# Score matmuls of a gated cross-attention block, addressed as 64-row array tiles

## The chip, the cores and the metric

The kernel runs on one core of one Trainium2 chip. The metric is the device time of one execution in microseconds (us), as the median of several runs. All arrays are float32.

## The reference

The reference is one block of a Flamingo-like model: layer norm, cross-attention to a context with a small feed-forward, a gated residual, layer norm, a top-2 mixture of eight experts with a shared one, a gated residual. B=4, N=512 query rows, 1601 context rows, width 256, context width 192, 16 heads of 16.

```python
def xattn(x, y):                      # x (4,512,256) normalised, y (4,1601,192)
    q = (x @ Wq + bq).reshape(B, N, 16, 16)
    k = (y @ Wk + bk).reshape(B, M, 16, 16)
    v = (y @ Wv + bv).reshape(B, M, 16, 16)
    scores = einsum('bnhd,bmhd->bhnm', q, k) / 4
    attn = softmax(scores, axis=-1)
    out = einsum('bhnm,bmhd->bnhd', attn, v).reshape(B, N, 256)
    return relu(out @ W1 + b1) @ W2 + b2
x = x + tanh(g_xattn) * xattn(layernorm(x), ctx)
x = x + tanh(g_ffn) * moe(layernorm(x))   # shared + top 2 of 8 experts, silu-gated, 256 -> 512 -> 256
```

## The kernel before

The kernel has two blocks, `attention` and `experts`; the change lies in the first. Attention works through 16 **units**, each one batch element and four heads, and each unit through 13 **steps**, one key tile of 128 context rows each: 208 steps.

**Stacks.** The scores are computed in fp32r with a high and a low part of q and k. For each pair p of heads, `kst` holds three parts of 16 rows for head 2p from partition 0 on and for head 2p+1 from partition 64 on (`[128, 2, 1604]`, filled with ones outside the parts), and `qst` the query side, one plane per head (`[128, 4, 512]`), with zeros in the rows of the other head, so that a matmul over all 128 rows gives one head's scores. Row 48 of a head's part (`STK`) takes the negated row maximum of q, against the ones of `kst`. Three buffers of each rotate (`NKB`). `load_stacks` on SP's queue writes them by 28 small DMAs a unit: 12 for kst (L310), 12 for qst (L312), and 4 that set row 48 to zero from `zrow` (L317). `load_rows` (L324) writes the maxima later.

**Two passes over the scores.** First, `S` jobs (L488): for each head, query tile t and key quarter q, 128 queries by 402 keys into one bank of the four-bank `ring`, 64 chunks a unit; VectorE takes the maximum of each (L677) and frees the slot. Then a `MX` job transposes the maxima, which go to row 48. Second, `st` (L542): 128 keys by 512 queries of one head into one of the three banks `st_ps`; ScalarE writes the exponential to `probs` (L442). `pv` (L554) multiplies the four heads' `probs` of a step by the values, on four column tiles of 32, into one accumulating bank `pv_ps`, with a column of ones for the denominator.

**Order.** `schedule()` writes the order by hand. The chunks of unit u+1 are spread over the steps of unit u, five in most steps, shifted by LEAD = 3 steps; the chunks of unit 0 and the first 15 of unit 1 stand in the prologue. The other jobs (K, Q, V projections and transposes XT of the next batch element; SUM, DIV, W1, W2 of the last) are put in fixed steps and all use the ring, in one order of slots: job n waits until job n-4 is freed. In a step TensorE's order is: chunk, st h0, chunk, st h1, chunk, st h2, `pv` of the step before, chunk, st h3, then what is left of the chunks, then the others.

```python
def st(u, mt, h):                                    # L536
    if idx >= NST:
        pe.wait_ge(exp_done, idx - NST + 1)          # three banks
def pv(m):                                           # L545
    pe.wait_ge(exp_done, 4 * (m + 1))                # all four heads of its step
```

In the K and V jobs the contraction over the context's width 192 is split in 128 and 64 rows. SP's queue works in its own order (L334 to L346): at the start of unit u the stacks of u+2, then `pack(u-1)` (L295), which W1 waits for, then the maxima of u+1.

Of the kernel before, what the change touches and what calls it, by code (L numbers as in the profile page):

```python
# [22 lines left out]
F32 = mybir.dt.float32  # L23
# [52 lines left out]
def schedule():  # L76

    def proj(b):
        return ([("XT", b, dt) for dt in range(2)] + [("Q", b, dt) for dt in range(2)],
                [("K", b, dt, q) for dt in range(2) for q in range(4)],  # L80
                [("V", b, g) for g in range(VJOBS)])

    def scores(u):
        return [("S", u, h, t, q) for h in range(4) for t in range(NT) for q in range(4)]


    qj, k, v = proj(0)

    prologue = k + qj + v + scores(0) + [("MX", 0)]
    jobs = [[] for _ in range(UNITS * MT)]  # L90
    for u in range(1, UNITS):
        chunks, start = scores(u), MT * (u - 1) - LEAD
        for n, chunk in enumerate(chunks):
            at = start + n * MT // len(chunks)
            if at < 0:
                prologue.append(chunk)
            else:
                jobs[at].append(chunk)
        jobs[start + MT].append(("MX", u))
    for u in range(UNITS):  # L100
        b, hg = divmod(u, 4)
        extra = {}
        if u > 0:
            extra[1], extra[2] = [("SUM", u - 1)], [("DIV", u - 1)]
        if u == UNITS - 1:
            for n in range(B - 1):
                extra[7 + 2 * n] = [("XT2", n, 0), ("XT2", n, 1)]
                extra[8 + 2 * n] = [("LG", n)]
        if hg == 0 and b > 0:
            for f in range(F1 // P):  # L110
                extra[5 + f] = [("W1", b - 1, f)]
            extra[10], extra[11] = [("W2", b - 1, 0)], [("W2", b - 1, 1)]
        if b + 1 < B:
            qj, k, v = proj(b + 1)
            if hg == 1:
                extra[3], extra[5], extra[6] = qj[0:2], qj[2:3], qj[3:4]
                for n in range(5):
                    extra[8 + n] = k[n:n + 1]
            if hg == 2:
                extra[0] = k[5:6]  # L120
                extra[1], extra[3] = extra[1] + k[6:7], k[7:8]
                for n in range(VJOBS):
                    extra[4 + n] = v[n:n + 1]
        for mt, more in extra.items():
            jobs[MT * u + mt] += more

    steps = [(m // MT, m % MT, sorted(jobs[m], key=lambda job: job[0] != "S")) for m in range(UNITS * MT)]
    b = B - 1
    epilogue = ([("SUM", UNITS - 1), ("DIV", UNITS - 1)] + [("W1", b, f) for f in range(F1 // P)] +
                [("W2", b, 0), ("W2", b, 1)])  # L130
    return prologue, steps, epilogue
# [47 lines left out]
def attention(nc, I, x1, stats, mv, veps, power, rstd, tg, ident, xg_dram,  # L179
# [19 lines left out]
    with ExitStack() as ctx:  # L199
# [26 lines left out]
        kc = parts[:, 4 * N:4 * (N + MP)].rearrange("p (t c n) -> p t c n", t=2, c=2).bitcast(F32R)  # L226
        vp = sb("vp", [P, 2, MT, H, VW])
        kst = [sb(f"kst{i}", [P, 2, MP], F32R) for i in range(NKB)]
        qst = [sb(f"qst{i}", [P, 4, N], F32R) for i in range(NKB)]
        zrow = sb("zrow", [4, P])  # L230
        zeros = sb("zeros", [P, D])
        mpart = sb("mpart", [P, 4, NT, 4])
        mx = sb("mx", [P, 4, NT])
# [29 lines left out]
        zeroed = sem("zeroed")  # L263

        QK_LOADS, W_LOADS = 5, 11
        STACK_LOADS = 16 * 2 * 7
        block = ctx.enter_context(nc.Block())

        @block.sync
        def _(sp):  # L270
# [26 lines left out]
            def load_stacks(u):  # L297
                b, hg = divmod(u, 4)

                sp.wait_ge(ring_free, max(count(("K", b, 1, 3)), count(("Q", b, 1))))  # L300
                if u >= NKB:
                    sp.wait_ge(st_full, 4 * MT * (u - NKB + 1))
                for p in range(2):
                    loaded = stack_loaded[u % NKB][p]
                    for j in range(2):
                        head = 4 * hg + 2 * p + j
                        dt, r = head // 8, HD * (head % 8)
                        for g, (qpart, kpart) in enumerate(((0, 0), (0, 1), (1, 0))):
                            at = 64 * j + HD * g
                            sp.dma_start(kst[u % NKB][at:at + HD, p, :].bitcast(F32),  # L310
                                         kc[r:r + HD, dt, kpart, :].bitcast(F32)).then_inc(loaded, 16)
                            sp.dma_start(qst[u % NKB][at:at + HD, 2 * p + j, :].bitcast(F32),  # L312
                                         qc[r:r + HD, dt, qpart, :].bitcast(F32)).then_inc(loaded, 16)


                        at = 64 * j + STK
                        sp.dma_start(qst[u % NKB][at:at + 1, 2 * p + j, :].rearrange("o (t n) -> o t n", n=P).bitcast(F32),  # L317
                                     zrow[:]).then_inc(loaded, 16)

            def load_rows(u):  # L320
                sp.wait_ge(ring_free, count(("MX", u)))
                for h in range(4):
                    at = 64 * (h % 2) + STK
                    sp.dma_start(qst[u % NKB][at:at + 1, h, :].rearrange("o (t n) -> o t n", n=P).bitcast(F32),  # L324
                                 mneg[NT * h:NT * (h + 1), :].bitcast(F32)).then_inc(row_loaded[u % NKB], 16)

            sp.wait_ge(pool_ready, 5)
# [24 lines left out]
        def _(pool):  # L352
# [6 lines left out]

            nc.gpsimd.affine_select(out=sel[:], in_=sel[:], compare_op=ALU.not_equal, fill=1.0, base=-HD,  # L360
                                    pattern=[[-32, 4]], channel_multiplier=1).then_inc(pool_ready, 1)
            nc.gpsimd.memset(zrow[:], 0.0)
            nc.gpsimd.memset(zeros[:], 0.0)
            nc.gpsimd.memset(vp[:, :, :, :, HD:VW].rearrange("p c m h o -> p (c m h) o"), 1.0)
            for i in range(NKB):
                nc.gpsimd.memset(qst[i][:].bitcast(F32), 0.0)
                last = nc.gpsimd.memset(kst[i][:].bitcast(F32), 1.0)
            last.then_inc(pool_ready, 1)
            def make_rstd(b):
# [81 lines left out]
        def _(pe):  # L451
            def do(job):
# [31 lines left out]
                elif kind == "S":  # L484
                    _, u, h, t, q = job
                    if h % 2 == 0 and (t, q) == (0, 0):
                        pe.wait_ge(stack_loaded[u % NKB][h // 2], STACK_LOADS * (u // NKB + 1))
                    last = nc.tensor.matmul(slot[:, 0:SCH], qst[u % NKB][:, h, t * P:(t + 1) * P],  # L488
                                            kst[u % NKB][:, h // 2, score_at(q):score_at(q) + SCH],
                                            start=True, stop=True)  # L490
                elif kind == "MX":
                    pe.wait_ge(mx_ready, job[1] + 1)
# [43 lines left out]
            def st(u, mt, h):  # L536
# [2 lines left out]
                    pe.wait_ge(row_loaded[u % NKB], 64 * (u // NKB + 1))  # L539
                if idx >= NST:  # L540
                    pe.wait_ge(exp_done, idx - NST + 1)
                nc.tensor.matmul(st_ps[0:w, idx % NST, :], kst[u % NKB][:, h // 2, mt * P:mt * P + w],  # L542
                                 qst[u % NKB][:, h, :], start=True, stop=True).then_inc(st_full, 1)

            def pv(m):  # L545
                u, mt = divmod(m, MT)
# [15 lines left out]
            for u, mt, jobs in steps:  # L562

                chunks = [job for job in jobs if job[0] == "S"]
                others = [job for job in jobs if job[0] != "S"]
                for h in range(4):
                    if h == 3 and MT * u + mt > 0:
                        pv(MT * u + mt - 1)
                    for job in chunks[h:h + 1]:
                        do(job)  # L570
                    st(u, mt, h)
                for job in chunks[4:] + others:
                    do(job)
            pv(MT * UNITS - 1)
            for job in epilogue:
# [577 lines left out]
```

## Time and profile before

| | us |
|---|---|
| median of 3 runs | 1333.47 |
| lowest, highest | 1330.21, 1335.7 |
| span of the profiled execution | 1354.8 |
| TensorE busy in it (5662 matmuls) | 1254.9 |
| VectorE busy | 749.8 |
| ScalarE busy | 546.8 |

The profile is of one execution, which with a span of 1354.8 us is longer than the median of the runs by 21 us; of its own time outside the span nothing is recorded. PE is TensorE's matmuls, PEld its weight loads, DVE VectorE, ACT ScalarE, POOL GpSimd, SPq the DMA issues of the sync engine. A matmul's recorded duration contains its way through the array, so that matmuls which follow one on another overlap in the record; the distance between their starts is what each holds the engine. "Idle before" is the engine's idle time ahead of an instruction, with what ended it. The lines of the view by rows join instructions of one group that stand close to each other.

### The profile page before, as it was taken

How to read it: one execution, taken by the hardware profiler on the slowest of the kernel's cores; microseconds unless marked ns; L12 is line 12 of the kernel's file. 1: busy time of each engine (PE TensorE's matmuls, PEld its weight loads, DVE VectorE, ACT ScalarE, POOL GpSimd, SP SyncE). 2: the span in 40 equal slices, each digit the busy share in tenths (PEclk: the TensorE clock that was granted, in tenths of full speed). 3: DMA queues.
4: the chain of work that ended last, by engine and by line, in shares of the span. 5: the costliest groups of instructions: out<-in, count | busy, mean ns of one | idle time of the engine just before them, and what ended most of it. 6: DMA issues, size and time to landing. Idle time of an engine off the chain costs nothing. (4 is left out here: it accounts for less than half of the span.)

```text
span 1354.8 us, 16247 instructions
## 1 busy us (share of the span) xinstructions
PE 1254.9 (93%) x5662; PEld 704.1 (52%) x5662; DVE 749.8 (55%) x1624; ACT 546.8 (40%) x1004; POOL 97.3 (7%) x114
## 2 busy tenths in 40 slices
PE   6899999999999999999999999997858999999982
PEld 2455545555645555554555565544434555555551
DVE  1498776686776588576668778632601222222244
ACT  1006564564555366346456547771201111111110
POOL 4000000000000000000000000000170000000044
PEclk9959999999999999899999999997988999999996
DMA  9344403323210453040322421010850111111124
GB/s 308 45 68 71 53 1 47 63 37 51 28 26 1 53 90 49 5 53 1 41 32 34 53 30 24 5 51 4 297 184 31 32 46 40 39 48 39 39 71 124
DMA packets 53840, 78.43 MB, mean 58 GB/s; under 512 B 13312, under 2 KB 38912, under 8 KB 53760
## 3 DMA queue, kind: packets, MB, share of 16 engines
q1 hardware_dynamic: 47744, 67.01, 24.9%
q0 software_dynamic: 3072, 8.39, 1.9%
q10 hardware_dynamic: 2944, 1.98, 0.5%
q8 instruction: 47, 0.77, 0.2%
q14 instruction: 33, 0.27, 0.1%
HBM read 32.47 MB, written 16.52 MB: 36 GB/s over the span
## 5 line engine op out<-in xcount | busy, mean ns | idle before, releaser
L442 ACT ACTIVATE probs<-st_ps 128x512 f32<-128x512 f32 (+1 forms) x832 | 450.5, 598 | 361.8 <-PE st_ps L542 360.6
L677 DVE TENSOR_REDUCE mpart<-ring 128x1 f32<-128x402 f32 x1024 | 521.3, 568 | 85.0 <-PE ring L488 83.0
L488 PE MATMUL ring<-kst,qst 128*128 128x402 f32 x1024 | 389.1, 406 | 0.8 <-DVE xnT L637 0.3
L542 PE MATMUL st_ps<-qst,kst 128*128 128x512 f32 (+1 forms) x832 | 327.7, 400 | 1.9 <-ACT probs L442 1.8
L488 PEld LDWEIGHTS ring<-kst,qst 128*128 128x128 f32 x1024 | 200.1, 196 | 215.1 <-DVE mpart L677 175.9
L554 PE MATMUL pv_ps<-probs,vp 128*17 128x512 f32 (+1 forms) x1664 | 219.6, 600 | 0.1
L542 PEld LDWEIGHTS st_ps<-qst,kst 128*128 128x128 f32 (+1 forms) x832 | 154.0, 187 | 41.8 <-ACT probs L442 19.5
L845 ACT ACTIVATE s_sb<-gu_ps 128x512 f32<-128x512 f32 x55 | 32.9, 598 | 304.8 <-PE gu_ps L920 252.5
L920 PE MATMUL gu_ps<-wgu,xbT 128*128 x312 | 144.1, 604 | 7.4 <-issue 7.3
L1049 DVE TENSOR_TENSOR h_sb<-s_sb,gu_ps 128x512 f32<-128x512 f32 x55 | 37.8, 687 | 204.0 <-ACT s_sb L845 184.0
L920 PEld LDWEIGHTS gu_ps<-wgu,xbT 128*128 128x128 f32 x312 | 56.1, 189 | 78.5 <-issue 78.5
L473 PE MATMUL ring<-cold,wk 64*128 64x401 f32 (+1 forms) x128 | 67.3, 633 | 10.2 <-DMA bq<-in_bq 10.2
L939 PE MATMUL y_ps<-wd,hT 128*128 x312 | 73.9, 380 | 0.0
L382 POOL COPY rspread<-rden 128x512 f32<-128x512 f32 x16 | 9.8, 616 | 841.6 <-DVE rden L688 841.6
L939 PE MATMUL y_ps<-cold,hT 128*128 128x256 f32 x128 | 37.3, 443 | 31.6 <-DVE x L1063 17.9
L482 PE MATMUL ring<-wv,cold 128*128 128x256 f32 (+1 forms) x208 | 64.2, 417 | 0.0
L920 PE MATMUL gu_ps<-cold,parts 128*128 128x512 f32 x128 | 60.7, 620 | 2.0 <-PEq L199 2.0
L554 PEld LDWEIGHTS pv_ps<-probs,vp 128*17 128x17 f32 (+1 forms) x1664 | 27.6, 95 | 66.2 <-ACT probs L442 57.0
L939 PEld LDWEIGHTS y_ps<-wd,hT 128*128 128x128 f32 x312 | 56.2, 190 | 6.0
L656 DVE SCALAR_TENSOR_TENSOR parts<-ring,bk,parts 128x401 fp32r<-128x401 f32 x32 | 20.3, 635 | 59.3 <-ACT parts L427 59.3
L835 POOL DMA_INDIRECT y_back<-sorted_y,slot_i x32 | 31.2, 975 | 295.4 <-DMA sorted_y<-ysb 279.1
L928 PEld LDWEIGHTS ht_ps<-ident,h_sb 128*128 128x128 f32 x220 | 27.7, 142 | 38.0 <-issue 27.4
(125 smaller groups left out, 716.2 us busy)
## 6 DMA issues: line engine op xcount, KB each, us to landing
kst<-parts SPq DMA_DIRECT2D x192, 100.2 KB
qst<-parts SPq DMA_DIRECT2D x192, 32.0 KB
sorted_x<-zeros SPq DMA_DIRECT2D x1, 4992.0 KB, 16.4
xb<-sorted_x SPq DMA_DIRECT2D x39, 128.0 KB, 2.1
sorted_y<-ysb SPq DMA_DIRECT2D x39, 128.0 KB, 1.7
wgu<-in_WgT SPq DMA_DIRECT2D x16, 256.0 KB, 6.7
wgu<-in_WuT SPq DMA_DIRECT2D x16, 256.0 KB, 7.1
wd<-in_WdT SPq DMA_DIRECT2D x8, 512.0 KB, 8.4
```

Of the source, the lines that this page charges most:

```text
L442: nc.scalar.activation(probs[0:w, m % NPB, h, :], st_ps[0:w, (4 * m + h) % NST, :], ACT.Exp, scale=SCALE).then_inc(exp_done, 1)
L473: last = nc.tensor.matmul(slot[:, 0:KCH], w[:, dt * P:(dt + 1) * P], c[:, q * KCH:(q + 1) * KCH], start=(k == 0), stop=(k == 1))
L482: last = nc.tensor.matmul(slot[0:w, i * D:(i + 1) * D], c[:, mt * P:mt * P + w], wv[:, :], start=(k == 0), stop=(k == 1))
L488: last = nc.tensor.matmul(slot[:, 0:SCH], qst[u % NKB][:, h, t * P:(t + 1) * P], kst[u % NKB][:, h // 2, score_at(q):score_at(q) + SCH], s ...
L542: nc.tensor.matmul(st_ps[0:w, idx % NST, :], kst[u % NKB][:, h // 2, mt * P:mt * P + w], qst[u % NKB][:, h, :], start=True, stop=True).the ...
L554: last = nc.tensor.matmul(pv_ps[32 * h:32 * h + VW, :], vp[0:w, b % 2, mt, 4 * hg + h, :], probs[0:w, m % NPB, h, :], start=(mt == 0), sto ...
L677: last = nc.vector.tensor_reduce(mpart[:, h, t, q:q + 1], slot[:, 0:SCH], AX.X, ALU.max)
L835: pool.indirect_dma_start(yg[:, n % NYG, c, :], None, yg_dram[:], bass.IndirectOffsetOnAxis(ap=slot_i[:, c, t:t + 1], axis=0)).then_inc(ga ...
L845: nc.scalar.activation(s_sb[:, i % 2, :], gu_ps[:, i % 2, 0, :], ACT.Silu).then_inc(silu_done, 1)
L920: last = nc.tensor.matmul(gu_ps[:, i % 2, f, :], x, w, start=(k == 0), stop=(k == 1))
L939: last = nc.tensor.matmul(y_ps[:, 0:D], hT[:, i % 2, k, :], w, start=(k == 0), stop=(k == FK - 1))
L1049: nc.vector.tensor_tensor(h_sb[:, i % 2, :], s_sb[:, i % 2, :], gu_ps[:, i % 2, 1, :], ALU.mult).then_inc(h_ready, 1)
```

## The change

Query stacks of a pair of heads now share one plane, `qst` is `[128, 2, 512]`, with head 2p in rows 0 to 47 (48 with the maximum) and head 2p+1 in rows 64 to 111 (112). Every score matmul names only its head's rows: 48 in `S`, which leaves row 48 out, and 49 in `st`. So they are addressed to the array's 64-row tiles at row 0 and row 64. The zero rows, the zeroing DMAs and the memset of `qst` are gone. The chunks of a pair of heads alternate between the two, and in a step the order is: two chunks, st h0 and h1, two chunks, st h2 and h3, the chunks left, `pv` of the step before, the others. The chunks' size, their banks and VectorE's maxima are as before.

```diff
     def scores(u):
-        return [("S", u, h, t, q) for h in range(4) for t in range(NT) for q in range(4)]
+        return [("S", u, 2 * p + j, t, q) for p in range(2) for t in range(NT) for q in range(4) for j in range(2)]
...
-        qst = [sb(f"qst{i}", [P, 4, N], F32R) for i in range(NKB)]
-        zrow = sb("zrow", [4, P])
+        qst = [sb(f"qst{i}", [P, 2, N], F32R) for i in range(NKB)]
...
-        STACK_LOADS = 16 * 2 * 7
+        STACK_LOADS = 16 * 2 * 6
...
-                        at = 64 * j + STK
-                        sp.dma_start(qst[u % NKB][at:at + 1, 2 * p + j, :].rearrange("o (t n) -> o t n", n=P).bitcast(F32),
-                                     zrow[:]).then_inc(loaded, 16)
...
             for i in range(NKB):
-                nc.gpsimd.memset(qst[i][:].bitcast(F32), 0.0)
...
-                    last = nc.tensor.matmul(slot[:, 0:SCH], qst[u % NKB][:, h, t * P:(t + 1) * P],
-                                            kst[u % NKB][:, h // 2, score_at(q):score_at(q) + SCH],
+                    at = 64 * (h % 2)
+                    last = nc.tensor.matmul(slot[:, 0:SCH], qst[u % NKB][at:at + STK, h // 2, t * P:(t + 1) * P],
+                                            kst[u % NKB][at:at + STK, h // 2, score_at(q):score_at(q) + SCH],
                                             start=True, stop=True)
...
-                nc.tensor.matmul(st_ps[0:w, idx % NST, :], kst[u % NKB][:, h // 2, mt * P:mt * P + w],
-                                 qst[u % NKB][:, h, :], start=True, stop=True).then_inc(st_full, 1)
+                at = 64 * (h % 2)
+                rows = slice(at, at + STK + 1)
+                nc.tensor.matmul(st_ps[0:w, idx % NST, :], kst[u % NKB][rows, h // 2, mt * P:mt * P + w],
+                                 qst[u % NKB][rows, h // 2, :], start=True, stop=True).then_inc(st_full, 1)
...
-                for h in range(4):
-                    if h == 3 and MT * u + mt > 0:
-                        pv(MT * u + mt - 1)
-                    for job in chunks[h:h + 1]:
+                for p in range(2):
+                    for job in chunks[2 * p:2 * p + 2]:
                         do(job)
-                    st(u, mt, h)
-                for job in chunks[4:] + others:
+                    for j in range(2):
+                        st(u, mt, 2 * p + j)
+                for job in chunks[4:]:
+                    do(job)
+                if MT * u + mt > 0:
+                    pv(MT * u + mt - 1)
+                for job in others:
                     do(job)
```

TensorE's order in plain steps of unit 0, before (chunks are `ring<-kst,qst`, key-major scores `st_ps<-qst,kst`, weighted values `pv_ps<-probs,vp`):

```order
49 L554 MATMUL pv_ps<-probs,vp 17x512 x4
50 L488 MATMUL ring<-kst,qst 128x402
51 L542 MATMUL st_ps<-qst,kst 128x512
52 L488 MATMUL ring<-kst,qst 128x402 x2
53 L542 MATMUL st_ps<-qst,kst 128x512
54 L488 MATMUL ring<-kst,qst 128x402
55 L542 MATMUL st_ps<-qst,kst 128x512
56 L488 MATMUL ring<-kst,qst 128x402
57 L542 MATMUL st_ps<-qst,kst 128x512
58 L554 MATMUL pv_ps<-probs,vp 17x512 x4
```

and after the change:

```order
41 L549 MATMUL pv_ps<-probs,vp 17x512 x4
42 L481 MATMUL ring<-kst,qst 128x402 x2
43 L537 MATMUL st_ps<-qst,kst 128x512 x2
44 L481 MATMUL ring<-kst,qst 128x402 x2
45 L537 MATMUL st_ps<-qst,kst 128x512 x2
46 L481 MATMUL ring<-kst,qst 128x402
47 L549 MATMUL pv_ps<-probs,vp 17x512 x4
```

Between two pv groups stand the same five chunks and four key-major matmuls; before, the first of the latter behind pv was h3 of the step, and now all four of a step stand together.

TensorE's order around a K projection (`ring<-cold,wk`) in unit 1, before:

```order
214 L554 MATMUL pv_ps<-probs,vp 17x512 x4
215 L488 MATMUL ring<-kst,qst 128x402
216 L542 MATMUL st_ps<-qst,kst 128x512
217 L488 MATMUL ring<-kst,qst 128x402
218 L473 MATMUL ring<-cold,wk 128x401 x2
219 L488 MATMUL ring<-kst,qst 128x402
220 L542 MATMUL st_ps<-qst,kst 128x512
```

and after:

```order
141 L481 MATMUL ring<-kst,qst 128x402
142 L549 MATMUL pv_ps<-probs,vp 17x512 x4
143 L465 MATMUL ring<-cold,wk 128x401 x2
144 L481 MATMUL ring<-kst,qst 128x402 x2
145 L537 MATMUL st_ps<-qst,kst 128x512 x2
```

The projection stood behind h3 and the last chunk, with pv before those; now pv stands directly before it.

## Rows read from the trace of the kernel before

**Rows 1.** Windows: us, busy (x) of PE, PEld, DVE, ACT, POOL, PEclk, DMA

```profile
286.00:307.00 21.00, 21.00 (x120) 11.51 (x119) 17.43 (x37) 14.93 (x29) 0.00 (x0) 1.00 0.12 14
888.00:912.00 24.00, 23.13 (x143) 11.14 (x146) 12.30 (x43) 17.36 (x33) 3.17 (x3) 1.00 0.03 6
```

**Rows 2.** The page's costliest groups: xcount | busy us, mean ns | idle before

```profile
L442 ACT ACTIVATE probs<-st_ps 128x512 f32<-128x512 f32 (+1 forms) x832 | 450.5, 598 | 361.8 <-PE st_ps L542 360.6
L677 DVE TENSOR_REDUCE mpart<-ring 128x1 f32<-128x402 f32 x1024 | 521.3, 568 | 85.0 <-PE ring L488 83.0
```

**Rows 3.** Timeline of a plain step, unit 3: start us, us, engine, line

```profile
289.28 0.13 PEld L554 LDWEIGHTS pv_ps<-probs,vp 128*17 128x17 f32 x8 [0.32 <-ACT probs L442]
289.28 1.05 PE L554 MATMUL pv_ps<-probs,vp 128*17 128x512 f32 x8
290.26 0.19 PEld L488 LDWEIGHTS ring<-kst,qst 128*128 128x128 f32 x1 [0.85 <-DVE mpart L677]
290.37 0.19 PEld L542 LDWEIGHTS st_ps<-qst,kst 128*128 128x128 f32 x1
290.55 0.39 PE L542 MATMUL st_ps<-qst,kst 128*128 128x512 f32 x1
...
290.98 1.68 ACT L442 ACTIVATE probs<-st_ps 128x512 f32<-128x512 f32 x3 [0.84 <-PE st_ps L542]
...
291.38 0.34 PE L488 MATMUL ring<-kst,qst 128*128 128x402 f32 x1
...
291.56 0.39 PE L542 MATMUL st_ps<-qst,kst 128*128 128x512 f32 x1
...
291.79 0.35 PE L488 MATMUL ring<-kst,qst 128*128 128x402 f32 x1
...
291.98 0.39 PE L542 MATMUL st_ps<-qst,kst 128*128 128x512 f32 x1
292.29 0.13 PEld L554 LDWEIGHTS pv_ps<-probs,vp 128*17 128x17 f32 x8 [0.31 <-ACT probs L442]
```

**Rows 4.** Timeline of a step with a K projection, unit 2

```profile
217.61 0.29 PEld L473 LDWEIGHTS ring<-cold,wk 64*128 64x128 f32 x2 [0.57 <-issue]
218.48 0.19 PEld L488 LDWEIGHTS ring<-kst,qst 128*128 128x128 f32 x1 [0.57 <-issue]
...
219.28 0.63 DVE L656 SCALAR_TENSOR_TENSOR parts<-ring,bk,parts 128x401 fp32r<-128x401 f32 x1 [1.59 <-ACT parts L427]
```

**Rows 5.** Timeline of the prologue, VectorE's chunks of unit 0

```profile
64.25 31.03 DVE L677 TENSOR_REDUCE mpart<-ring 128x1 f32<-128x402 f32 x64
```

**Rows 6.** Timeline of a step without chunks, unit 15

```profile
898.39 2.07 ACT L442 ACTIVATE probs<-st_ps 128x512 f32<-128x512 f32 x4 [0.52 <-PE st_ps L542]
899.04 0.19 PEld L542 LDWEIGHTS st_ps<-qst,kst 128*128 128x128 f32 x1 [0.66 <-ACT probs L442]
...
899.47 0.13 PEld L554 LDWEIGHTS pv_ps<-probs,vp 128*17 128x17 f32 x8 [0.24 <-ACT probs L442]
```

**Rows 7.** Groups by line: VectorE's work on W2

```profile
L701 DVE TENSOR_TENSOR ytmp<-ring,b 128x256 f32<-128x256 f32 x16 | 6.0, 419 | 21.0 <-PE ring L532 21.0
```

**Rows 8.** Timeline of SP's queue, unit 4

```profile
303.10 0.56 SPq L310 DMA_DIRECT2D kst<-parts  x1
...
320.84 0.63 SPq L317 DMA_DIRECT2D qst<-zrow  x1
321.51 2.41 SPq L295 DMA_DIRECT2D onc<-on  x4
```

**Rows 9.** Who waited for whom: us in total, times, longest us

```profile
PE ring L524 <- DMA onc<-on: 11.0, 4, 4.6
...
PE ring L462 <- DVE xn L606: 9.2, 4, 2.8
```

**Rows 10.** Windows, columns as in rows 1: behind W1's wait, unit 8

```profile
544.60:551.40 6.80, 6.15 (x14) 3.32 (x18) 2.22 (x4) 1.27 (x3) 0.00 (x0) 0.50 0.00 1
```

**Rows 11.** Timeline of TensorE in unit 1, at the lower clock

```profile
160.89 1.71 PE L554 MATMUL pv_ps<-probs,vp 128*17 128x512 f32 x8
```

More of the change, by code:

```diff
@@ L311, in load_stacks @@
                                          kc[r:r + HD, dt, kpart, :].bitcast(F32)).then_inc(loaded, 16)
-                            sp.dma_start(qst[u % NKB][at:at + HD, 2 * p + j, :].bitcast(F32),
+                            sp.dma_start(qst[u % NKB][at:at + HD, p, :].bitcast(F32),
                                          qc[r:r + HD, dt, qpart, :].bitcast(F32)).then_inc(loaded, 16)
-                        at = 64 * j + STK
-                        sp.dma_start(qst[u % NKB][at:at + 1, 2 * p + j, :].rearrange("o (t n) -> o t n", n=P).bitcast(F32),
-                                     zrow[:]).then_inc(loaded, 16)
             def load_rows(u):
@@ L323, in load_rows @@
                     at = 64 * (h % 2) + STK
-                    sp.dma_start(qst[u % NKB][at:at + 1, h, :].rearrange("o (t n) -> o t n", n=P).bitcast(F32),
+                    sp.dma_start(qst[u % NKB][at:at + 1, h // 2, :].rearrange("o (t n) -> o t n", n=P).bitcast(F32),
                                  mneg[NT * h:NT * (h + 1), :].bitcast(F32)).then_inc(row_loaded[u % NKB], 16)
@@ L361, in _ @@
                                     pattern=[[-32, 4]], channel_multiplier=1).then_inc(pool_ready, 1)
-            nc.gpsimd.memset(zrow[:], 0.0)
             nc.gpsimd.memset(zeros[:], 0.0)
```

## The prediction

> **What bounds the kernel now.** I first read windows [rows 1]. In a stretch of plain steps of the attention loop (208 steps: 16 units of 13 key tiles) TensorE is busy all of 21 us, VectorE 17.4, ScalarE 14.9. The prologue is touched in little and the experts not at all, so the loop decides. The costliest groups [rows 2] are the two that read the scores: VectorE reduces the chunks (L677), ScalarE exponentiates the key-major tiles (L442, 598 ns); TensorE makes them in L488 and L542 and multiplies with the values in L554 (pv).
>
> The timeline of one plain step [rows 3] has no hole on TensorE. From one pv group (289.28) to the next (292.29) it is 3.01 us: pv holds the engine for 0.98 (289.28 to 290.26), and nine matmuls follow one on another. A score chunk takes 0.18 (291.38 to 291.56), a key-major one 0.23 (291.56 to 291.79), each load (PEld) under the matmul before it. At pv's two edges something is lost: pv starts 0.32 after the last key-major matmul, not 0.23, and the first chunk behind it needs 0.29 instead of 0.18, as its load (290.26) could not run early: the next load starts 0.11 after it (290.37). I read this as the price of a change of tile shape: about 0.10 at the end of the old shape and 0.11 for an uncovered load, 0.2 together. The K projection confirms it inside a job: its 64-row half changes shape, its load starts only at 217.61, and the first chunk's load behind it again only at 218.48 [rows 4].
>
> VectorE takes a chunk every 0.48 (31.03 us for 64 in the prologue [rows 5]), 2.4 a step. ScalarE takes a tile about every 0.5. So TensorE is the bound by about 0.6 us a step, and the question is what its program order makes wait once it is faster.
>
> **The change part by part. 1: the plain step.** Two matmuls on rows 0 and 64 use different halves of the array and write different banks, so I expect them to run together. TensorE's own work would fall from 3.01 to about 2.1. But the new order has a chain in it. The key-major matmul h3 must wait for the exponential of h0 (three banks), and pv, which used to fill that wait, now stands behind h3. This chain is priced from the steps without chunks [rows 6], where it shows today. Start at the first chunk's load behind pv: loads one behind another each 0.11 put h0 at 0.33; from a key-major start to its exponential 0.43 (290.55 to 290.98 [rows 3]); exponential 0.60; its end (898.39 + 0.60) to the next load 0.05 (899.04); that load to pv 0.43 (899.04 to 899.47); pv 0.98. Sum 2.82. In about every second step the five chunks begin on row 64, since five is odd. Then the second chunk shares h0's rows (h0 at 0.40) and the fifth shares h3's and runs behind it (0.17): 3.06. Mean 2.94 against 3.01, that is -0.07 in the 192 steps that have chunks: **-13 us**.
>
> The unknown is whether the two halves' loads run together. The nearest rows both ways: 0.11 apart (full array), or hardly apart, as pv's eight loads on four column tiles, which take 0.13 in all. With the second, h0 is at 0.29 and pv earlier: 2.78 and 2.95, -0.14 a step. If nothing overlaps at all, h0 starts at 0.29 + 0.18 = 0.47, the step is 2.96, and the fifth chunk's 0.18 on top makes 3.14: +0.13. I take the first, since here too both loads bring 128 columns each, and keep the others for the range.
>
> The Trainium skill (page "TensorE: Matmul & The Clock Gate", section "The mechanism") says that loads and matmuls on different row groups start about 4 ns apart. By it the step would be the second value, 2.87. No row of this trace has two row tiles in flight, so the rule is a rival below.
>
> **2: changes of shape.** K and V end in their 64-row half. Today they cost: into 64 rows, and out of it to the full array. After the change the chunk that follows is in 64-row shape already; but pv now stands before them, another edge only if they need the full array first. Counted over a step, K had four edges (chunk to pv, pv to chunk, into, out of) and will have three (to pv, pv to K, K's inner one): -0.2 in the 45 steps with K or V in the written order, **-9 us**. Jobs in the full array alone (SUM, DIV, MX, Q, W1, W2, XT) stand in 57 other steps with chunks; they had two edges and get three: **+11 us**. V alternates twice and still saves one.
>
> **3: the ring.** All five chunks of a step now stand before its pv, and there are four ring slots. The fifth chunk waits until VectorE has reduced the first one of the same step. In a plain step it has (0.29 + 0.2 + 0.48, under 1.5). Behind K it hasn't: K's low part ends on VectorE 1.43 after K's end (219.28 + 0.63 against 218.48 [rows 4]), the first chunk's reduction 0.48 later, so the fifth chunk starts at about 1.95 and pv at about 2.35, where the chain alone has pv at 1.84 to 2.08. I take 0.45 for 24 K steps (+11). Q's two passes are 0.1 longer each: 0.6 for 6 (+3.5). Behind W2 VectorE has two adds of 0.42 [rows 7] and two operations of the same shape: fifth chunk at 2.4, 0.65 for 6 (+4). **+18 us**. Ends: 0 if ScalarE and VectorE come sooner, +30. Today the fourth and fifth chunk come behind pv and wait for none of this.
>
> **4: the last unit.** Its steps have no chunks; today SUM, DIV, the second transposes and LG fill the wait for the exponential (0.66 of idle before the load at 899.04 [rows 6]). Now they stand outside it. Eight or nine such jobs at 0.4 to 0.7: **+5 us**.
>
> **5: waits that shrink.** SP issues 28 stack transfers at the start of a unit, 18.4 us (303.10 to 321.51), and only then the pack that W1 waits for [rows 8]. Four of them, the zero rows (0.63 each), go: 2.6 earlier. And pv, 0.98, now runs before W1 instead of behind it. Together 3.6. The list of waits has W1 four times behind the pack, 11.0 in all [rows 9]; the longest, 4.6, is the epilogue's, so units 4, 8 and 12 share 6.4, none of them over 3.6: -6.5. Behind the wait in unit 8 the granted clock is 0.50 for 6.8 us [rows 10]; without two such dips I take -4. XT's wait for the normalised rows (up to 2.8 [rows 9], three times in the loop) has pv before it and saves about 1 each: -3.5. **-14 us**. The memsets of qst and zrow on POOL gate only the first stack transfers, which wait for the K and Q projections anyway: nothing. The other 16 x 4 zero-row transfers lie under other work; in the prologue VectorE's 0.48 per chunk is the bound [rows 5]: nothing. Were that cover gone, each transfer would cost its 0.63.
>
> Sum: -13 - 9 + 11 + 18 + 5 - 14 = **-2 us**. The profiled execution spans 1354.8, 21 above the median 1333.47; the terms are differences of durations at full clock, so I take them off the median: **1331 us**. Here 0.5% (6.7 us) is about what a measurement can tell from no change.
>
> **The rivals.** *Loads together.* The halves' loads overlap as pv's do: another -0.07 in the 159 steps without the ring's wait, -11: **1320 us**. For it: pv's loads, and the skill's sentence. Against: pv's have 17 columns each.
>
> *No overlap, the slower side.* Row tiles run one behind another (a shared read path or load buffer). Then only the order has changed: the chain plus the serial chunks, 0.20 more than the forecast in those 159 steps: +32, **1363 us**. It decides as soon as a pair of key-major matmuls starts over 0.15 apart. For it: full-array matmuls never overlap here. Against: pv's four column tiles do (eight matmuls of 512 columns in 1.05, where eight at 0.23 would take 1.84). This is also the case in which the change doesn't do what it says.
>
> *The clock.* TensorE will idle about 0.45 a step. If the grant fell to 1.2 GHz in a third of the loop, a step would cost about 1.1 more (pv alone 1.71 instead of 1.05 at 160.89 [rows 11]): +70, **1400 us**. Against: in the last unit it waits 0.66 in each step of 2.6 and has 1.00 granted [rows 1].
>
> **How the numbers follow.** Forecast 0.60 (own range 1314 to 1345: the ring term from 0 to 30 and term 5), loads together 0.20, no overlap 0.12, clock 0.05, else 0.03. Range 1306 to 1364: loads together with a small ring term at the low end, no overlap at the high. Faster by over 0.5%: a third of the forecast and most of the second case, 0.35. Within: half the forecast and some of the second, 0.35. Slower: the rest of the forecast, no overlap, clock: 0.30.
>
> **What would show it.** In the plain steps of the new trace: pairs of L481 and of L537 with starts 0.11 apart or less; a hole before each h3, ended by ScalarE; steps of 2.8 and 3.05 in turn. In K steps the fifth chunk released by VectorE. W1 without a wait for the pack. VectorE and ScalarE groups unchanged in mean. Plain steps under 2.7 would mean that the chain is not what I think; over 3.1, that nothing overlaps.

## The result and the profile after

| | before | changed |
|---|---|---|
| median, us | 1332.74 (4 runs) | 1439.94 (4 runs) |
| lowest, highest | 1330.21, 1335.7 | 1423.31, 1446.3 |
| ratio | | 1.075, 95% interval 1.069 to 1.082 |
| span of the profiled execution | 1354.8 | 1444.6 |
| mean granted clock in it | 0.958 | 0.866 |

The change is slower by 7.5%, 107 us by the medians, and outside the range that was given. The profiled execution of the changed kernel is the slowest of its four; the others have a mean granted clock of 0.871 to 0.884. The spans of the two profiles differ by less than the medians, since the experts behind the loop took 18 us more in that of before, from the same instructions. In the traces of all runs below they take either 412 to 416 or 431 to 434 us, whatever the kernel, so this is no effect of the change. The attention loop alone, by windows of the two traces (columns: us, then busy and count of PE, PEld, DVE, ACT and POOL, granted clock, DMA share, GB/s), before:

```profile
107.00:922.00 815.00, 799.98 (x4193) 443.95 (x4189) 570.25 (x1183) 471.04 (x871) 14.33 (x21) 0.99 0.25 36
```

and changed, with two stretches out of it, one of unit 7 and one that begins two steps before unit 13 and ends in it:

```profile
109.00:1030.00 921.00, 852.10 (x4190) 378.43 (x4186) 563.20 (x1182) 454.40 (x871) 14.27 (x21) 0.84 0.22 32
549.90:583.40 33.50, 30.64 (x198) 12.49 (x196) 29.48 (x60) 24.29 (x48) 0.00 (x0) 1.00 0.17 24
874.20:935.60 61.40, 61.40 (x235) 25.12 (x227) 33.71 (x69) 26.08 (x51) 0.61 (x1) 0.50 0.22 29
```

The loop is 106 us longer, the whole loss. Its granted clock is 0.84 instead of 0.99. As the grant has two levels, 1.2 and 2.4 GHz, a mean c says that the share 2(1-c) was spent at the lower: 0.32 of 921, about 295 us, against 16 before (with two digits of c, such figures are good to about 9 us either way). The two stretches hold plain steps in the main (the second also those with SUM and DIV): at 2.4 GHz 60 VectorE operations pass in 33.5 us (0.56 each), at 1.2 GHz 69 in 61.4 (0.89). Plain steps alone say the same. In the second stretch, from one pv group to the next:

```profile
895.39 1.91 PE L549 MATMUL pv_ps<-probs,vp 128*17 128x512 f32 x8
900.10 1.91 PE L549 MATMUL pv_ps<-probs,vp 128*17 128x512 f32 x8
904.47 1.91 PE L549 MATMUL pv_ps<-probs,vp 128*17 128x512 f32 x8
```

They take 4.71 and 4.37 in turn, 4.54 on average, against 2.87 at the full clock (below). So a us at the lower level loses 0.37 us, 295 lose 109, and that is the loss. At the full clock the changed loop would take about 812, and that of before 809, by the same sum.

A plain step of it in unit 7, timeline at the full clock (start us, us, engine, line):

```profile
564.28 0.19 PEld L481 LDWEIGHTS ring<-kst,qst 48*128 48x128 f32 x2 [0.85 <-DVE mpart L675]
564.28 0.46 PE L481 MATMUL ring<-kst,qst 48*128 48x402 f32 x2
564.39 0.19 PEld L537 LDWEIGHTS st_ps<-qst,kst 49*128 49x128 f32 x2
564.57 0.40 PE L537 MATMUL st_ps<-qst,kst 49*128 49x512 f32 x2
...
565.00 2.06 ACT L434 ACTIVATE probs<-st_ps 128x512 f32<-128x512 f32 x4 [0.72 <-PE st_ps L537]
565.65 0.18 PEld L537 LDWEIGHTS st_ps<-qst,kst 49*128 49x128 f32 x1 [0.65 <-ACT probs L434]
565.65 0.49 PE L537 MATMUL st_ps<-qst,kst 49*128 49x512 f32 x1 [0.27 <-ACT probs L434]
565.76 0.19 PEld L481 LDWEIGHTS ring<-kst,qst 48*128 48x128 f32 x1
565.99 0.34 PE L481 MATMUL ring<-kst,qst 48*128 48x402 f32 x1
566.26 0.13 PEld L549 LDWEIGHTS pv_ps<-probs,vp 128*17 128x17 f32 x8 [0.31 <-ACT probs L434]
566.26 1.05 PE L549 MATMUL pv_ps<-probs,vp 128*17 128x512 f32 x8
567.24 0.19 PEld L481 LDWEIGHTS ring<-kst,qst 48*128 48x128 f32 x2 [0.85 <-DVE mpart L675]
```

Two key-major matmuls take 0.40 in one record, where a single one has 0.39 [rows 3] and two on the full array have 0.62 (run 1 below); the two chunks behind pv take 0.46 with their uncovered load, where run 1 has 0.64; two loads take 0.19, as one does. So the pair runs together, loads too. From first load to first load it is 2.96 us; the next step of the same trace takes 2.78 (567.24 to 570.02). The chain is there link by link: h0 at 0.29, its exponential 0.43 later (565.00), the load of h3 at 565.65 with 0.65 of idle before it that ScalarE ended, pv 0.61 later, 0.98 for pv.

The groups that answer to [rows 2], and TensorE's three, on the changed kernel's page:

```profile
L434 ACT ACTIVATE probs<-st_ps 128x512 f32<-128x512 f32 (+1 forms) x832 | 433.5, 600 | 426.6 <-PE st_ps L537 426.3
L675 DVE TENSOR_REDUCE mpart<-ring 128x1 f32<-128x402 f32 x1024 | 513.4, 568 | 61.1 <-PE ring L481 59.9
L481 PE MATMUL ring<-kst,qst 48*128 48x402 f32 x1024 | 348.2, 479 | 36.3 <-DVE parts L654 20.3
L549 PE MATMUL pv_ps<-probs,vp 128*17 128x512 f32 (+1 forms) x1664 | 265.3, 715 | 0.0
```

ScalarE's and VectorE's means are as before (600 and 568 ns). Those of TensorE grew with the clock: pv was not touched, and its mean is 715 ns. Where the grant falls shows in a step that has SUM, unit 8, timeline:

```profile
584.44 1.05 PE L490 MATMUL ring<-sel,osb 128*128 128x4 f32 x8
...
587.42 1.90 PE L549 MATMUL pv_ps<-probs,vp 128*17 128x512 f32 x8
```

SUM moves 4 columns eight times in 1.05 us; the pv at the end of this step already takes 1.90 instead of 1.05. This is one place of many: other stretches at the lower level begin where no SUM stands near (the longest, from 874.20 on, 10 us before the SUM of unit 13 at 884.34).

### The profile page after: what moved, and what is told of

It reads as the page before. It is cut to its first block and busy times, and to the rows that moved or that the text cites. A ratio compares the mean times of both kernels' runs of the same rounds, so it can differ in the third digit from the quotient of the medians.

```text
span 1444.6 us, 16179 instructions
## 1 busy us (share of the span) xinstructions
PE 1305.0 (90%) x5662; PEld 637.3 (44%) x5662; DVE 743.5 (51%) x1624; ACT 530.2 (37%) x1004; POOL 91.6 (6%) x110
## 5 line engine op out<-in xcount | busy, mean ns | idle before, releaser
L434 ACT ACTIVATE probs<-st_ps 128x512 f32<-128x512 f32 (+1 forms) x832 | 433.5, 600 | 426.6 <-PE st_ps L537 426.3
L481 PE MATMUL ring<-kst,qst 48*128 48x402 f32 x1024 | 348.2, 479 | 36.3 <-DVE parts L654 20.3
L537 PE MATMUL st_ps<-qst,kst 49*128 49x512 f32 (+1 forms) x832 | 301.2, 474 | 27.8 <-ACT probs L434 27.1
L549 PE MATMUL pv_ps<-probs,vp 128*17 128x512 f32 (+1 forms) x1664 | 265.3, 715 | 0.0
L481 PEld LDWEIGHTS ring<-kst,qst 48*128 48x128 f32 x1024 | 168.8, 215 | 206.4 <-DVE mpart L675 93.1
L537 PEld LDWEIGHTS st_ps<-qst,kst 49*128 49x128 f32 (+1 forms) x832 | 135.5, 209 | 109.4 <-ACT probs L434 96.4
L465 PE MATMUL ring<-cold,wk 64*128 64x401 f32 (+1 forms) x128 | 82.8, 760 | 10.3 <-DMA bq<-in_bq 10.3
L654 DVE SCALAR_TENSOR_TENSOR parts<-ring,bk,parts 128x401 fp32r<-128x401 f32 x32 | 20.3, 635 | 86.3 <-ACT parts L419 86.3
L465 PEld LDWEIGHTS ring<-cold,wk 64*128 64x128 f32 (+1 forms) x128 | 26.8, 261 | 65.0 <-issue 47.2
L474 PEld LDWEIGHTS ring<-wv,cold 128*128 128x128 f32 (+1 forms) x208 | 32.3, 194 | 47.8 <-issue 32.0
L419 ACT ACTIVATE parts<-ring,bk 128x401 fp32r<-128x401 f32 x32 | 19.0, 595 | 85.4 <-PE ring L465 85.3
```

What stands on the lines that cost most here:

```text
L434: nc.scalar.activation(probs[0:w, m % NPB, h, :], st_ps[0:w, (4 * m + h) % NST, :], ACT.Exp, scale=SCALE).then_inc(exp_done, 1)
L465: last = nc.tensor.matmul(slot[:, 0:KCH], w[:, dt * P:(dt + 1) * P], c[:, q * KCH:(q + 1) * KCH], start=(k == 0), stop=(k == 1))
L474: last = nc.tensor.matmul(slot[0:w, i * D:(i + 1) * D], c[:, mt * P:mt * P + w], wv[:, :], start=(k == 0), stop=(k == 1))
L481: last = nc.tensor.matmul(slot[:, 0:SCH], qst[u % NKB][at:at + STK, h // 2, t * P:(t + 1) * P], kst[u % NKB][at:at + STK, h // 2, score_at ...
L537: nc.tensor.matmul(st_ps[0:w, idx % NST, :], kst[u % NKB][rows, h // 2, mt * P:mt * P + w], qst[u % NKB][rows, h // 2, :], start=True, sto ...
L549: last = nc.tensor.matmul(pv_ps[32 * h:32 * h + VW, :], vp[0:w, b % 2, mt, 4 * hg + h, :], probs[0:w, m % NPB, h, :], start=(mt == 0), sto ...
```

## Experiments

Theory A: the loss is TensorE's clock, and it falls because the 64-row tiles leave the array with less work per us. Theory B: the new order brings it, by pv's place and the hole in front of h3.

**1. The order alone.** The kernel before, with only the changed step loop; chunks stay in their order by heads.

```diff
-                for h in range(4):
-                    if h == 3 and MT * u + mt > 0:
-                        pv(MT * u + mt - 1)
-                    for job in chunks[h:h + 1]:
+                for p in range(2):
+                    for job in chunks[2 * p:2 * p + 2]:
                         do(job)
-                    st(u, mt, h)
-                for job in chunks[4:] + others:
+                    for j in range(2):
+                        st(u, mt, 2 * p + j)
+                for job in chunks[4:]:
+                    do(job)
+                if MT * u + mt > 0:
+                    pv(MT * u + mt - 1)
+                for job in others:
                     do(job)
```

> The kernel before (full-array matmuls, its chunk order by heads) with only the new order of a step: two chunks, h0 and h1, two chunks, h2 and h3, the chunks left, pv, the others. Theory A (the time was lost to TensorE's clock, which falls because 64-row tiles leave the array with less work per us): full-array matmuls keep it busy, the loop has under 40 us at 1.2 GHz as before (17), and the time rises only by the order's own chain, a plain step 3.1 instead of 3.01: about 1365 us. Theory B (the new place of pv brings the clock down by its holes): some 200 to 300 us of the loop at 1.2 GHz here too, time over 1420 us.

Measured: ratio 1.024 (1.021 to 1.027), 1387.2 us beside 1355.3 for before on the same chip. Window of its loop:

```profile
108.00:952.00 844.00, 821.85 (x4188) 427.00 (x4186) 561.08 (x1181) 456.29 (x872) 14.28 (x21) 1.00 0.24 35
```

and out of the timeline of a plain step:

```profile
290.82 0.64 PE L488 MATMUL ring<-kst,qst 128*128 128x402 f32 x2
291.29 0.62 PE L542 MATMUL st_ps<-qst,kst 128*128 128x512 f32 x2
...
292.37 0.19 PEld L542 LDWEIGHTS st_ps<-qst,kst 128*128 128x128 f32 x1 [0.25 <-ACT probs L442]
...
293.96 0.64 PE L488 MATMUL ring<-kst,qst 128*128 128x402 f32 x2
```

The clock is full, better than before: the order alone does not bring it down, so Theory B falls. The order has its own price, 29 us of the loop (844 against 815): its plain steps take 3.14 (290.82 to 293.96), which is the value that the prediction gave for the case without overlap, and the load of h3 has the hole before it that ScalarE ends.

**2. The tiles alone.** The changed kernel's tiles, stacks and transfers in the order of before.

```diff
+        return [("S", u, h, t, q) for h in range(4) for t in range(NT) for q in range(4)]
...
+                for h in range(4):
+                    if h == 3 and MT * u + mt > 0:
+                        pv(MT * u + mt - 1)
...
```

> The changed kernel's 64-row tiles and small stacks, with the order of before in both respects (chunks by heads, a chunk and a key-major matmul in turn, pv before h3). Theory A: less array work per us than before, so the clock falls as in the changed kernel, 200 us or more of the loop at 1.2 GHz, over 1400 us. Theory B: the clock stays as before (under 40 us low) and neighbouring tiles overlap where they can: at full clock a plain step of about 2.6, 1280 to 1300 us.

Measured: ratio 0.990 (0.987 to 0.993), 1340.7 beside 1355.3. Window:

```profile
108.00:906.00 798.00, 779.70 (x4189) 378.47 (x4188) 567.51 (x1183) 466.27 (x872) 14.29 (x21) 0.93 0.25 37
```

Neither theory's number came. The clock falls with the tiles alone (about 110 us low), as A says, but by a third of the changed kernel's, and the steps gain more than that costs: the loop is 17 us shorter than before. So it is the tiles that bring the clock down, and tiles and new order together that bring it down so far. By the sum above (0.37 us for each at the lower level) this loop would take about 757 at the full clock, 52 less than that of before; the changed order, at about 812, gives all of it back.

**3. pv back before h3, chunks still in pairs.**

```diff
+                    for j in range(2):
+                        if (p, j) == (1, 1) and MT * u + mt > 0:
+                            pv(MT * u + mt - 1)
+                        st(u, mt, 2 * p + j)
```

> The changed kernel with pv put back before h3, chunks still in pairs. Theory A: TensorE does the same work in shorter steps (2.7 at full clock), so its share of busy time rises somewhat; the clock still falls in part, 1300 to 1400 us. Theory B: no hole before h3, clock as before, about 1290 us.

Measured: 1496.7 and 1533.1 us beside 1355.3, slower by over 10%; both executions are far above the changed kernel's. The profile is that of the longer one, with a mean clock of 0.801; the other had 0.827. Window of its loop, and of plain steps in it at the full clock:

```profile
109.00:1098.00 989.00, 942.17 (x4194) 413.46 (x4196) 569.45 (x1182) 468.24 (x872) 14.31 (x21) 0.74 0.20 30
622.00:649.00 27.00, 25.61 (x170) 10.39 (x169) 24.49 (x51) 20.54 (x40) 0.00 (x0) 1.00 0.16 21
```

A miss for both theories by about 100 us and more. Over half of this loop is at 1.2 GHz. Is idle time what brings the clock down? The lower level itself makes TensorE's busy share larger (61.40 of 61.40 us in the stretch above), so the share has to be compared at the full clock: in plain steps TensorE is busy 25.61 of 27.00 us here (95%) and 30.64 of 33.50 in the changed kernel (91%). Less idle time went with the lower clock, so idle time is not what decides. Why this order is so much worse is open.

**4. Work added.** The changed kernel, each matmul of h2 issued twice into the same bank.

```diff
+                if h == 2:
+                    nc.tensor.matmul(st_ps[0:w, idx % NST, :], kst[u % NKB][rows, h // 2, mt * P:mt * P + w],
+                                     qst[u % NKB][rows, h // 2, :], start=True, stop=True)
```

> The changed kernel with each key-major matmul of h2 issued twice into the same bank (same result), which lies in the hole before h3: 208 matmuls more. Theory A: more array work per us, the clock recovers at least in part: under 200 us of the loop at 1.2 GHz (changed kernel 300), time 1330 to 1400 us although work is added. If instead the loss has another cause than the clock, the added 0.2 us a step costs 0 to 40 us: 1440 to 1480 us.

Measured: ratio 1.034 (1.031 to 1.038), 1401.4 beside 1355.3, against the changed kernel's 1.075. With 208 matmuls more the ratio is lower by 4%, as Theory A had it:

```profile
108.00:965.00 857.00, 809.70 (x4396) 377.87 (x4392) 561.27 (x1181) 457.36 (x871) 14.31 (x21) 0.92 0.23 34
```

About 137 us of it are at the lower level. At the full clock it would take some 806, so the added matmuls cost nothing: they fill the hole before h3.

**5. More rows.** What does "work" mean here? The changed kernel again, with 64 rows named by every score matmul instead of 48 or 49; the rows added hold zeros on the query side and ones on the key side. For that the four zero-row transfers of a unit and the memset of `qst` are back too.

```diff
-                    last = nc.tensor.matmul(slot[:, 0:SCH], qst[u % NKB][at:at + STK, h // 2, t * P:(t + 1) * P],
-                                            kst[u % NKB][at:at + STK, h // 2, score_at(q):score_at(q) + SCH],
+                    last = nc.tensor.matmul(slot[:, 0:SCH], qst[u % NKB][at:at + 64, h // 2, t * P:(t + 1) * P],
+                                            kst[u % NKB][at:at + 64, h // 2, score_at(q):score_at(q) + SCH],
...
-                rows = slice(at, at + STK + 1)
+                rows = slice(at, at + 64)
...
+                        sp.dma_start(qst[u % NKB][at:at + 1, p, :].rearrange("o (t n) -> o t n", n=P).bitcast(F32),
+                                     zrow[:]).then_inc(loaded, 16)
...
+                nc.gpsimd.memset(qst[i][:].bitcast(F32), 0.0)
```

> The changed kernel with the same tiles, order and timing, but each score matmul names 64 rows instead of 48 or 49 (the extra rows hold zeros on the query side; the zero-row transfers and the memset are back). If what holds the clock up is how much of the array takes part, a third more rows must recover part of it: under 200 us of the loop at 1.2 GHz (changed kernel 300), under 1400 us. If only the time counts in which matmuls stream, which halves when two run together, the rows change nothing: 300 us low or somewhat less or more, 1420 to 1460 us.

Measured: ratio 1.011 (1.004 to 1.018), 1351.9 beside 1336.0. Windows of its loop and of a stretch of unit 13, where the changed kernel was at the lower clock:

```profile
107.00:934.00 827.00, 744.73 (x4192) 333.20 (x4194) 561.88 (x1183) 454.21 (x871) 14.27 (x21) 0.97 0.25 35
814.00:849.00 35.00, 32.36 (x212) 13.32 (x210) 30.09 (x62) 24.69 (x49) 0.00 (x0) 1.00 0.19 26
```

TensorE has the same instructions in the same order, and at the full clock the loop would take about 809 beside 812; yet 94 us of it come back: 50 us low instead of 295. TensorE's busy share at the full clock is the same (32.36 of 35.00 us, 92%, against 91%). So the clock follows the rows that the matmuls name, or what the added rows hold; the two are not told apart.

**6. The dose.** 64 rows in the key-major matmuls alone; the chunks keep 48, and no zero rows are transferred.

```diff
+                nc.gpsimd.memset(qst[i][:].bitcast(F32), 0.0)
...
-                rows = slice(at, at + STK + 1)
+                rows = slice(at, at + 64)
```

> The changed kernel with 64 rows in the key-major matmuls alone (the chunks keep 48), 4 x 512 of the 4 x 512 + 5 x 402 columns of a step. With rows as the measure a dose between the changed kernel (300 us low) and rows64 (54): 100 to 220 us low, 1370 to 1410 us. If the zero-row transfers or the later pack of rows64 made its difference instead of the rows, nothing is gained here: 1420 us or more.

Measured: ratio 1.016 (1.007 to 1.024), 1375.8 beside 1353.6. Window of its loop:

```profile
109.00:933.00 824.00, 748.43 (x4190) 334.95 (x4186) 561.27 (x1181) 453.81 (x870) 14.31 (x21) 0.96 0.24 35
```

The gain does not come from the zero-row transfers of run 5. Is it a dose in between? The profiled execution, the faster of two, has 66 us low, less than the 100 expected at least; the other has a mean clock of 0.924 against its 0.940, some 45 us more. By the ratios, four of nine matmuls a step bring all that run 5 brought, as far as two executions of each can tell. The same edit on run 3's kernel, the slowest of all:

> Run rows_pv_mid (506 us of its loop at 1.2 GHz, the slowest of all) with 64 rows instead of 49 in the key-major matmuls. If rows are what decides, most of it comes back here too: under 200 us low, under 1400 us. If that kernel's long stretches at the lower clock have another cause (pv between the key-major matmuls): still over 350 us low, over 1450 us.

Measured: 1372.4 beside 1349.6, ratio 1.017 (1.002 to 1.032), where run 3 had 1.10 to 1.13; this is the outcome that was expected if rows decide. Its loop:

```profile
109.00:945.00 836.00, 774.29 (x4192) 344.32 (x4188) 568.28 (x1181) 464.90 (x870) 14.27 (x21) 0.94 0.24 35
```

The runs stand beside before on the chip of each; the changed kernel itself was measured on one chip alone. Run 3 and its counterpart here were on two chips as well. That the chip should make 0.84 or 0.74 out of 0.96 is not tested away, but before has a mean clock of 0.958 to 0.966 on all of them.

**7. SUM.** The changed kernel with SUM's passes moving 128 columns.

```diff
-                        last = nc.tensor.matmul(slot[:, 4 * t:4 * t + 4], osb[:, t * P:(t + 1) * P],
+                        last = nc.tensor.matmul(slot[:, t * P:(t + 1) * P], osb[:, t * P:(t + 1) * P],
```

with `sel` 128 columns wide and the reciprocal reading four of each 128.

> The changed kernel with SUM's eight passes moving 128 columns instead of 4 (124 of them unused), at the same spacing, since each is bound by its weight load. Theory A: the falls of the clock at the starts of the units, where SUM stands and the array streams nearly nothing for 1 us, go or get shorter; 200 to 250 us of the loop at 1.2 GHz, 1390 to 1430 us. If SUM has nothing to do with it: no difference to the changed kernel beyond 10 us.

Measured: ratio 1.037 (1.022 to 1.053). Window of its loop:

```profile
109.00:962.00 853.00, 779.05 (x4192) 345.16 (x4194) 562.22 (x1182) 453.85 (x871) 14.26 (x21) 0.93 0.23 34
```

Some 120 us are low in this, the faster of two executions (1378.2 and 1395.5 us, mean clocks 0.924 and 0.906). That is more than was expected of one job of 1 us in each unit. How much of it is SUM's own doing isn't shown: low stretches are gone that do not begin behind a SUM (that of 874.20 among them), and in the old order the same edit brings nothing (run 8).

**8. The tiles in the order of before, with the remedies.** First SUM widened alone:

> The 64-row tiles in the order of before (run rows_old_order: 104 us of its loop at 1.2 GHz, 1 per cent faster than the kernel before) with SUM's passes widened to 128 columns. Theory A: its falls behind SUM and DIV in units 8, 13 and 14 (6.8 us each) go, 10 to 15 us less than rows_old_order; 2 per cent faster than the kernel before.

Measured: ratio 0.988 (0.977 to 1.000), loop clock 0.93 as in run 2: SUM brought nothing down there that could be seen, where 10 to 15 us were expected. With the second h2 matmul on top:

> As old_sum_wide, and each key-major matmul of h2 is issued twice. Theory A: the prologue's last stretch and the falls in units 1, 4, 5 and 9 get shorter too, under 60 us low in the loop; against it stands up to 0.2 us a step where TensorE is the bound: between 25 us faster and 20 us slower than old_sum_wide.

Measured: ratio 1.011 (1.000 to 1.022), 30 us slower than old_sum_wide and so outside what was expected. Its loop clock is better (0.95 against 0.93), but in this order no hole takes up the added matmuls, and they cost more than the clock gives. Then the rows, in all score matmuls (without the wide SUM) and in the key-major ones alone (with it):

> The order of before in both respects with 64-row tiles whose matmuls name all 64 rows (zero rows loaded as before). Theory A with rows as its measure (run rows64 had 54 us low instead of 300): the loop of rows_old_order (798 us) loses most of its 104 us at 1.2 GHz, about 40 us less, less the pack's wait that the 28 transfers bring back (7): ratio to the kernel before 0.96 to 0.975, 1280 to 1300 us on a chip where before takes 1333. If the rows' effect was chance: 0.985 to 1.0.

> As old_sum_wide, but the key-major matmuls name 64 rows (the chunks keep 48, so no zero-row transfers). Between old_sum_wide (0.988) and old_rows64: ratio 0.965 to 0.985, 50 to 90 us of the loop at 1.2 GHz.

Measured, three rounds: 0.983 (0.980 to 0.987) and **0.975 (0.970 to 0.979)**, 1332.0 and 1321.1 us beside 1353.6. The first is a smaller gain than expected, close to what was to be called chance (0.985 and above): 64 rows in all score matmuls bring 0.7% against run 2's 0.990, with W1's waits for the pack back. The second lies in its range, is better than the first by more than their intervals, and the best of all; it has the wide SUM and no zero-row transfers. Window of its loop:

```profile
108.00:888.00 780.00, 760.81 (x4194) 370.43 (x4197) 566.76 (x1183) 465.15 (x872) 14.33 (x21) 0.96 0.26 37
```

35 us less than before at a clock that is still below its 0.99. What the tiles save in this order (run 2) makes the larger part of it.

## Why the prediction was wrong

**The step that failed** is the rival called the clock: its chance of 0.05 and the reason against it. The prediction argued from the last unit, where TensorE waits in each step and has 1.00 granted [rows 1]. That row shows full-array matmuls with the same idle time; it says nothing of matmuls on 48 rows. Idle time was the wrong quantity, as runs 3 and 5 show; with 64 rows named, at the same idle time, the loop's clock is 0.97 instead of 0.84. Its price, 1.1 us for a plain step at the lower clock, was too low: 4.54 against 2.87 on average, 1.7. The pv of 1.71 that it was taken from [rows 11] was not at the lower level to its end:

```profile
158.90:162.30 3.40, 3.40 (x13) 0.99 (x12) 2.93 (x9) 1.79 (x3) 1.27 (x2) 0.50 0.49 69
162.40:163.00 0.60, 0.60 (x6) 0.47 (x3) 0.00 (x0) 0.00 (x0) 0.00 (x0) 1.00 0.24 55
```

It ends at 162.60; one wholly at the lower level takes 1.91. The rival's third of the loop was right (0.32), and that was a guess. So its 1400 us became 1440.

**The sum at the full clock** held: the terms gave -2 us, and the loops without their lost clock are about 812 and 809. It held in part by luck, since some terms were off and their errors cancel. With the loads as measured, the plain steps would have brought the sum to -13; K steps took back 3 us of that, and the rest isn't attributed.

- *Plain step*, forecast 2.82 and 3.06 in turn: 2.78 and 2.96. The chain is right in each link; the taken value for the loads was not. They start together (two in 0.19). The Trainium skill (page "TensorE: Matmul & The Clock Gate", section "The mechanism") has loads and matmuls on different row groups overlap, and the trace agrees. The 2.78 and 2.95 worked out for that case are what was measured. In the written terms the rival "loads together" was true and the serial one false. Its time of 1320 was not reached, for the clock.
- *Changes of shape*: right for V. A V step shortened from 5.53 (219.92 to 225.45, before) to 5.27 (501.09 to 506.36) between pv groups, where the terms gave -0.27.
- *The ring*: present and too small, and the job that waits is another one. In the list of waits of the changed kernel K's low part on VectorE ends idle time of loads and matmuls of the chunks; before, such rows do not stand in the list:

```profile
PEld ring L481 <- DVE mpart L675: 93.1, 179, 1.7
PEld ring L481 <- DVE parts L654: 30.5, 24, 1.4
PE ring L481 <- DVE parts L654: 20.3, 24, 1.0
...
PE ring L517 <- DMA onc<-on: 4.6, 1, 4.6
```

  24 times, once for each K step in the loop, 20.3 us on TensorE, where 11 were taken. The timeline of such a step:

```profile
216.50 1.05 PE L549 MATMUL pv_ps<-probs,vp 128*17 128x512 f32 x8
...
220.72 0.45 PE L481 MATMUL ring<-kst,qst 48*128 48x402 f32 x1 [1.00 <-DVE parts L654]
...
221.20 0.44 PE L481 MATMUL ring<-kst,qst 48*128 48x402 f32 x1
221.57 0.62 PE L549 MATMUL pv_ps<-probs,vp 65*17 65x512 f32 x4
```

  K holds a slot of the ring itself, so it is the fourth chunk behind it that waits, for K's own slot, and not the fifth for the first chunk's reduction. It holds up h2 and h3 with it. The step takes 5.07 (216.50 to 221.57) where before has 4.76 (196.09 to 200.85): +0.31, where the terms gave -0.07 - 0.2 + 0.45 = +0.18. The same wait behind V (17 times, 5.0 us on TensorE) has no term.
- *Waits that shrink*: right for the pack. Of four waits of W1 for the pack (11.0 us [rows 9]) the epilogue's 4.6 is left. In run rows64, where the zero-row transfers are back, the list has 11.0 in four again, so it is the transfers that shorten it and not pv's new place. The dips behind these waits are gone, but the clock now falls in many other places.
- *The order's price*, put at +0.13 a step for the case without overlap: run 1, where nothing can overlap, has it, 3.14 for 3.01.

## What to carry to other kernels

Splitting a matmul on few rows over row tiles saves TensorE time, but first see whether the clock holds: read the granted clock by stage before any busy time, and price an edit at both levels. Where the stage has little to spare, name all rows of the tile (zeros cost no matmul time here and brought back 94 us). A job of few columns may matter as well; widening it helped in one order and not in the other. And an order that groups the tiles must not put the filler of a wait behind the wait: the new order of a step cost 29 us on the full array (run 1), and with the tiles it gave back all that they save in the old one (run 2).

## What was not expected of the hardware

- The granted clock follows the rows that matmuls name, at equal timing: 0.84 in the loop with 48 and 49 rows, 0.97 with 64 in all score matmuls, 0.96 with 64 in the key-major ones alone; 0.74 and 0.94 for the order with pv before h3. Whether it is the rows named or the operands in them (zeros against ones were added) was not told apart; no run added rows with other data.
- It is not TensorE's busy share: in plain steps at the full clock 95% busy went with 0.74 in the loop, 91% with 0.84 and 92% with 0.97.
- The lower level can hold for long through work that runs at the full one elsewhere in the same kernel: 61 us in and before unit 13 with TensorE busy all of it, plain steps for the most part, while the same steps in unit 7 stay at 1.00. What decides between the two, and what part SUM has in it (run 7), is open; so is why the order of run 3 is so much worse than the changed one.
- The 64-row tiles' loads overlap fully: two loads of 128 columns in 0.19 us, as one.
